# Adjacency times signs, with residual and layer norm: quadrants' statistics combined by ScalarE copies and VectorE aggregation in place of TensorE sums

## The chip, the cores and the metric

The kernel runs on one core of one Trainium2 chip. The metric is the time of the program on the device in microseconds (us), lower is better. Runs of one kernel spread by some per cent here: the three of the kernel before go from 1036.94 to 1065.42.

## What is computed

```
x: (8192, 256)  adj: (8192, 8192), all float32, about 3 entries a row besides zeros  weight: (256, 256)
bw = sign(weight);  ba = max(sign(x), 0)
xw = ba @ bw.T                       # (8192, 256), small whole numbers
out = relu(adj @ xw)                 # the large product
y = x + out
result = (y - mean(y)) / sqrt(var(y) + 1e-5)     # over the 256 columns of each row
```

The product reads 268 MB of adj. It is made in two parts, hi and lo: hi is adj rounded to the matmul's type fp32r, lo the rest, and both are multiplied by xw and added up in the same bank.

## The kernel before, in words

The 8192 output rows are 16 blocks of 512 (`NBLK`, `b`). For each block the 8192 columns of adj are 8 chunks (`CH`), each of which is loaded by 4 DMAs of 512 KB, one to each quadrant of 32 partitions; a chunk is 4 units (`UPC`), so a block has 32 units (`UB`). Within a block `u` is the unit's number, `n` is counted over all blocks. Four chunk buffers (`SLOTS`) stand in `raw`.

One unit goes through this chain: VectorE transposes it in 32x32 squares (`turn`, L478), into `turned` (four buffers) or, for the ten "V" units of a block, into two PSUM banks; ScalarE converts it to hi (`make_hi`, L359); lo = turned - hi is made by GpSimd for the 22 "P" units (L339) and by VectorE for the V units (`make_lo`, L482); TensorE multiplies (`use_unit`, L685), 8 matmuls of 512 columns. hi and lo are rings of 6 (`RING`): `make_hi(n)` waits until TensorE has used unit n - 6. The V units are u = 0, 4, 7, 10, 13, 16, 20, 23, 26, 29 (in the first block 1 and 12 differ). Block b's sums stand transposed in two of four banks, which of the two pairs alternates with b.

The end of a block runs under the next block's units (`ending(b, u)`, b the finished block, u the unit of the one that runs). Each engine's order is the order of the code: unit's work first, then what `ending` has for that u. On VectorE: u = 7 transposes the two banks into `relu` (L511), u = 8 takes relu and adds the rows of x (L515), u = 9 to 12 make 16 `bn_stats`, four in each (L520). The rows are spread in quadrants: a partition holds 64 of a row's 256 columns (`rows_q`), so each row's statistics stand in four quadrants and have to be combined. TensorE does that after its unit 8 (`add_means`, L753: four matmuls with the matrix `quads`, which adds up over quadrants) and after its unit 16 (`add_vars`, L761), with small VectorE steps between (L524, L528, L532). ScalarE takes the root at u = 23 (L375), VectorE makes the scale and shift at 25 and 26 (L536, L539), and ScalarE normalises 16 groups of 64 columns, four in each of u = 27 to 30 (L380). `add_means` waits for all 16 `bn_stats`, on an engine whose order is fixed, so the products of unit 9 stand behind that wait.

DMAs are issued by SyncE (SP, the lower two quadrants of everything) and ScalarE (ACT, the upper two). Adjacency: `start_chunk`, L207; ScalarE issues one quadrant after unit n = 4(ch - 3) and the other one unit later. Rows of x are loaded by `load_quads` (L265, at u = 20 on ScalarE, behind a block's chunk 0 on SyncE) and the result stored by `store_quads` (L270, at u = 31 on ScalarE, behind chunk 3 on SyncE), 128 KB a quadrant, in packets of 256 bytes; the adjacency goes in packets of 1 KB. The last block is normalised in another way (`PIECES`), which the change leaves as it is.

## Time and profile before

| | us |
|---|---|
| median of 3 runs | 1051.39 |
| lowest, highest | 1036.94, 1065.42 |
| profiled execution | 1054.38 |
| its span, first to last instruction | 1052.6 |

| engine | busy us | share of the span |
|---|---|---|
| TensorE (PE) | 998.0 | 95% |
| its weight loads (PEld) | 819.0 | 78% |
| VectorE (DVE) | 898.8 | 85% |
| GpSimd (POOL) | 855.0 | 81% |
| ScalarE (ACT) | 638.7 | 61% |

The profile is that of one execution. Busy time is what an engine spends in instructions; two matmuls overlap in it, so TensorE's share is not a share of its peak, and the start of one matmul to the start of the next is the better measure. An instruction of TensorE, VectorE, ScalarE or GpSimd is named by engine, line and operation, output <- inputs. ACTq and SPq are the engines' own queues, in which a DMA's issue has a duration too. "Granted clock" is the share of TensorE's full clock of 2.4 GHz; 0.50 is its other level, 1.2 GHz. The rows of the sections below are printed as the profile has them.

### The profile page before, as it was taken

How to read it: one execution, taken by the hardware profiler on the slowest of the kernel's cores; microseconds unless marked ns; L12 is line 12 of the kernel's file. 1: busy time of each engine (PE TensorE's matmuls, PEld its weight loads, DVE VectorE, ACT ScalarE, POOL GpSimd, SP SyncE). 2: the span in 40 equal slices, each digit the busy share in tenths (PEclk: the TensorE clock that was granted, in tenths of full speed). 3: DMA queues.
4: the chain of work that ended last, by engine and by line, in shares of the span. 5: the costliest groups of instructions: out<-in, count | busy, mean ns of one | idle time of the engine just before them, and what ended most of it. 6: DMA issues, size and time to landing. Idle time of an engine off the chain costs nothing.

```text
span 1052.6 us, 12987 instructions
## 1 busy us (share of the span) xinstructions
PE 998.0 (95%) x4612; PEld 819.0 (78%) x4612; DVE 898.8 (85%) x1080; ACT 638.7 (61%) x807; POOL 855.0 (81%) x362
## 2 busy tenths in 40 slices
PE   6989999999999999999999999899998999999997
PEld 5978787887878787787877878688786887778776
DVE  6768979889898988979898897978979888798895
ACT  4777575565857457475665756547475664746565
POOL 3658978898898888879888897878879887888894
PEclk9999999999999999999999999999999999989999
DMA  9999999999999999999999999999999999999991
GB/s 303 349 331 324 272 298 291 267 308 277 301 284 299 294 258 282 274 293 292 289 316 258 292 282 288 280 244 289 277 292 290 281 295 274 274 269 263 304 205 40
DMA packets 344225, 294.74 MB, mean 280 GB/s; under 512 B 72544, under 2 KB 344160, under 8 KB 344160
## 3 DMA queue, kind: packets, MB, share of 16 engines
q1 hardware_dynamic: 172480, 147.35, 55.0%
q10 hardware_dynamic: 171680, 146.56, 53.9%
q8 instruction: 36, 0.59, 0.3%
q14 instruction: 29, 0.24, 0.1%
HBM read 285.47 MB, written 8.39 MB: 279 GB/s over the span
## 4 chain that ended last, share of the span: by engine, by line
DVE 34%; PE 34%; ACTq 11%; ACT 11%; issue 9%; POOL 0%; DVEq 0%; POOLq 0%
PE ps L685 29%; DVE turned L478 10%; DVE lo L482 9%; ACTq L207 8%; ACT hi L359 7%; DVE ps L478 7%; DVE stats_q L520 3%; ACTq L265 2%; ACT rows_e L380 2%; PE ps L679 2%; DVE relu L511 2%; DVE rows_e L515 1%; DVE rows L515 1%; ACT rows L380 1%; DVE dev_q L532 1%
## 5 line engine op out<-in xcount | busy, mean ns | idle before, releaser
L339 POOL TENSOR_TENSOR lo<-turned,hi 128x1024 fp32r<-128x1024 f32 x351 | 851.8, 2449 | 170.3 <-ACT hi L359 168.8
L685 PE MATMUL ps<-hi,xw 128*128 128x512 f32 x1984 | 786.5, 396 | 9.4 <-POOL lo L339 6.3
L685 PE MATMUL ps<-lo,xw 128*128 128x512 f32 x1984 | 780.3, 393 | 0.0
L359 ACT ACTIVATE hi<-turned 128x1024 fp32r<-128x1024 f32 x351 | 370.3, 1059 | 344.6 <-DVE turned L478 231.2
L685 PEld LDWEIGHTS ps<-hi,xw 128*128 128x128 f32 x1984 | 377.5, 190 | 96.7 <-POOL lo L339 15.0
L685 PEld LDWEIGHTS ps<-lo,xw 128*128 128x128 f32 x1984 | 377.3, 190 | 77.7
L478 DVE STREAM_TRANSPOSE turned<-raw 128x1024 f32<-128x1024 f32 x351 | 427.0, 1220 | 1.1 <-DMA raw<-in_adj_dram 1.1
L482 DVE TENSOR_TENSOR lo<-ps,hi 128x1024 fp32r<-128x1024 f32 x161 | 195.4, 1214 | 126.2 <-ACT hi L359 125.6
L478 DVE STREAM_TRANSPOSE ps<-raw 128x1024 f32<-128x1024 f32 x161 | 196.8, 1223 | 3.3 <-DMA raw<-in_adj_dram 3.0
L359 ACT ACTIVATE hi<-ps 128x1024 fp32r<-128x1024 f32 x161 | 164.5, 1022 | 42.2 <-DVE ps L478 30.8
L380 ACT ACTIVATE rows_e<-rows_e,shift_q,rstd_q 128x64 f32<-128x64 f32 x128 | 45.5, 428 | 0.0
L380 ACT ACTIVATE rows<-rows,shift_q,rstd_q 128x64 f32<-128x64 f32 x112 | 39.8, 428 | 0.0
L753 PE MATMUL ps<-stats_q,quads 128*128 128x16 f32 x60 | 10.4, 288 | 29.7 <-DVE stats_q L520 29.7
L753 PEld LDWEIGHTS ps<-stats_q,quads 128*128 128x128 f32 x60 | 8.9, 214 | 36.0 <-DVE stats_q L520 33.4
L679 PE MATMUL ps<-hi,xw 128*128 128x256 f32 x96 | 25.2, 300 | 0.1
L679 PE MATMUL ps<-lo,xw 128*128 128x256 f32 x96 | 24.6, 293 | 0.0
L532 DVE SCALAR_TENSOR_TENSOR dev_q<-sq_q,stats_q 128x32 f32<-128x32 f32 x15 | 24.5, 1631 | 0.0
L352 ACT ACTIVATE xw<-ps 128x1024 fp32r<-128x1024 f32 x16 | 16.4, 1025 | 9.8 <-PE ps L661 8.3
L679 PEld LDWEIGHTS ps<-hi,xw 128*128 128x128 f32 x96 | 19.4, 202 | 0.3 <-issue 0.3
L679 PEld LDWEIGHTS ps<-lo,xw 128*128 128x128 f32 x96 | 19.5, 203 | 0.0
L661 PE MATMUL ps<-sign_wT,rows 128*128 128x256 bf16 x128 | 17.9, 286 | 0.9 <-DVE rows L451 0.9
L511 DVE STREAM_TRANSPOSE relu<-ps 128x1024 f32<-128x1024 f32 x15 | 18.1, 1207 | 0.0
(54 smaller groups left out, 202.0 us busy)
## 6 DMA issues: line engine op xcount, KB each, us to landing
raw<-in_adj_dram SPq DMA_DIRECT2D x250, 512.0 KB, 10.8
raw<-in_adj_dram ACTq DMA_DIRECT2D x250, 512.0 KB, 12.6
raw<-in_adj_dram SPq DMA_DIRECT2D x12, 256.0 KB, 9.0
raw<-in_adj_dram ACTq DMA_DIRECT2D x12, 256.0 KB, 9.4
x_sb<-in_x_dram SPq DMA_DIRECT2D x10, 256.0 KB, 11.2
x_sb<-in_x_dram ACTq DMA_DIRECT2D x10, 256.0 KB, 11.6
rows_e<-in_x_dram ACTq DMA_DIRECT2D x16, 128.0 KB, 12.8
rows_e<-in_x_dram SPq DMA_DIRECT2D x16, 128.0 KB, 11.2
```

The lines of the kernel that those rows point to most:

```text
L207: eng.dma_start(raw_view(ch)[g * Q:(g + 1) * Q], adj_v[ch // CH, ch % CH, g]).then_inc(adj_loaded[ch % SLOTS], 16)
L265: eng.dma_start(rows_q[b % 2][q * Q:(q + 1) * Q], x_quads[b, q]).then_inc(quads_loaded[b % 2], 16)
L339: pool.tensor_tensor(lo[:, n % RING], turned[:, ordinal(n) % TP], hi[:, n % RING].bitcast(f32), ALU.subtract).then_inc(p_los_made, 1)
L359: act.activation(hi[:, n % RING], src, ACT.Copy).then_inc(his_made, 1)
L380: done = act.activation(row, row, ACT.Identity, bias=shift_q[:, t:t + 1], scale=rstd_q[:, t:t + 1])
L478: dve.transpose(dst.rearrange("p (k t j) -> p k t j", k=uk, j=Q), src).then_inc(units_turned, 1)
L482: dve.tensor_tensor(lo[:, n % RING], turned_v[:, :], hi[:, n % RING].bitcast(f32), ALU.subtract).then_inc(v_los_made, 1)
L511: dve.transpose(flat[0].rearrange("p (t a j) -> p a t j", t=NT, a=DH), pair[b % 2]).then_inc(sums_turned, 1)
L520: dve.bn_stats(stats_q[:, t], rows_q[b % 2][:, t]).then_inc(stats_made, 1)
L532: dve.scalar_tensor_tensor(out=dev_q[:], in0=sq_q[:], scalar=float(Q), in1=parts, op0=ALU.mult, op1=ALU.add).then_inc(parts_made, 1)
L679: return pe.matmul(acc[b % 2][a][:, n0:n0 + MB // 2], xw[:, step, a * P:(a + 1) * P], part[:, n % RING, k * MB // 2:(k + 1) * MB // 2], st ...
L685: return pe.matmul(acc[b % 2][a], xw[:, step, a * P:(a + 1) * P], part[:, n % RING, k * MB:(k + 1) * MB], start=(step == 0 and part is hi) ...
```

## The change

The line numbers of the changed kernel are some 15 lower on TensorE and some 8 higher on VectorE.

- TensorE's `add_means` and `add_vars`, the matrix `quads` and the small steps L524, L528 and L532 are gone.
- relu is taken by ScalarE in the banks themselves, after its hi of unit 5, two activations of 512 columns. VectorE transposes the banks at u = 6 (L518), not 7, and waits for that relu. At u = 7 the rows are added (L522) by a plain add.
- The 16 `bn_stats` are made two in each of u = 8 to 15 (L527).
- At u = 16 ScalarE copies the four quadrants' statistics side by side into partitions 0 to 31 (`near`, four copies of 16 x 6 numbers, L378). At u = 17 to 20 VectorE aggregates them, 16 `bn_aggr` on 24 numbers (L531). At u = 21 ScalarE takes the root and negates the mean (L381, L382), at u = 22 and 23 VectorE makes the reciprocal and the shift (L534, L538), at u = 24 ScalarE copies both back to all four quadrants (`scale_q`, four copies, L386).
- ScalarE normalises two or three groups in each of u = 25 to 31 (L391).
- SyncE alone loads and stores rows, four quadrants each time; ScalarE issues none.

```diff
+                if u == RING - 1:
+                    act.wait_ge(units_used, (b + 1) * UB)
+                    for a in range(DH):
+                        act.activation(acc[b % 2][a], acc[b % 2][a], ACT.Relu).then_inc(relus_made, 1)
+                if u == 16:
+                    act.wait_ge(stats_made, (b + 1) * NT)
+                    for q in range(G):
+                        act.activation(near[:, :, q], stats_q[q * Q:(q + 1) * Q], ACT.Copy).then_inc(stats_near, 1)
+                if u == 21:
+                    act.wait_ge(mvs_near, (b + 1) * NT)
+                    act.activation(std_q, mv_q[:, :, 1], ACT.Sqrt, bias=eps[0:Q]).then_inc(stds_made, 1)
+                    act.activation(neg_q, mv_q[:, :, 0], ACT.Copy, scale=-1.0).then_inc(negs_made, 1)
+                if u == 24:
+                    act.wait_ge(fins_made, b + 1)
+                    for q in range(G):
+                        act.activation(scale_q[q * Q:(q + 1) * Q], fin_q, ACT.Copy).then_inc(fins_spread, 1)
+                if u >= 25:
+                    act.wait_ge(fins_spread, (b + 1) * G)
+                    for t in range(NT * (u - 25) // 7, NT * (u - 24) // 7):
-                if u == 31:
-                    store_quads(act, b, UPPER)
-                if n % UB == 20 and n // UB < NBLK - 1:
-                    load_quads(act, n // UB, UPPER)
...
-                    dve.scalar_tensor_tensor(out=rows_q[b % 2], in0=back_q, scalar=0.0, in1=rows_q[b % 2],
-                                             op0=ALU.max, op1=ALU.add).then_inc(sums_made, 1)
-                if 9 <= u < 13:
+                    dve.tensor_tensor(rows_q[b % 2], flat[0].rearrange("p (t c) -> p t c", t=NT), rows_q[b % 2],
+                                      ALU.add).then_inc(sums_made, 1)
+                if 8 <= u < 16:
...
+                if 17 <= u < 21:
+                    dve.wait_ge(stats_near, (b + 1) * G)
+                    for t in range((u - 17) * G, (u - 16) * G):
+                        dve.bn_aggr(mv_q[:, t], near[:, t].rearrange("p q s -> p (q s)")).then_inc(mvs_near, 1)
...
-                if n >= UB and n % UB == MEANS_AT:
-                    add_means(n // UB - 1)
-                if n >= UB and n % UB == VARS_AT:
-                    add_vars(n // UB - 1)
```

TensorE's order at the end of unit 8 of the second block, before: the last products of unit 8, the matmuls of `add_means`, the first product of unit 9.

```order
L685 MATMUL ps<-hi,xw 128x512
L685 MATMUL ps<-lo,xw 128x512
L753 MATMUL ps<-stats_q,quads 128x16 x2
L685 MATMUL ps<-hi,xw 128x512
L685 MATMUL ps<-lo,xw 128x512
```

The L753 row, and after unit 16 an L761 row like it, stand nowhere in the changed order: unit 9 follows unit 8 directly.

VectorE's order from the transposition of the banks on (L511; `turned` and `ps` are the two places that L478 writes), before:

```order
L511 STREAM_TRANSPOSE relu<-ps 128x2x16x32 [waits sums_made,units_used]
L478 STREAM_TRANSPOSE turned<-raw 128x1024 [waits p_los_made,adj_loaded2]
L482 TENSOR_TENSOR lo<-ps,hi 128x1024 [waits his_made]
L515 SCALAR_TENSOR_TENSOR rows_e<-relu,rows_e 128x1024 [waits quads_loaded0,sums_turned]
L478 STREAM_TRANSPOSE turned<-raw 128x1024 [waits p_los_made]
L520 BN_STATS stats_q<-rows_e 128x6 [waits sums_made]
L520 BN_STATS stats_q<-rows_e 128x6 x3
L478 STREAM_TRANSPOSE ps<-raw 128x1024 [waits v_los_made]
```

And the same place now:

```order
L518 STREAM_TRANSPOSE relu<-ps 128x2x16x32 [waits fins_spread,relus_made]
L486 STREAM_TRANSPOSE ps<-raw 128x1024 [waits v_los_made]
L522 TENSOR_TENSOR rows_e<-relu,rows_e 128x1024 [waits quads_loaded0,sums_turned]
L486 STREAM_TRANSPOSE turned<-raw 128x1024 [waits p_los_made,adj_loaded2]
L490 TENSOR_TENSOR lo<-ps,hi 128x1024 [waits his_made]
L527 BN_STATS stats_q<-rows_e 128x6 [waits sums_made]
L527 BN_STATS stats_q<-rows_e 128x6
L486 STREAM_TRANSPOSE turned<-raw 128x1024 [waits p_los_made]
```

The transposition stands one unit earlier and waits for relus_made, and two statistics stand behind a unit where four stood.

ScalarE's order at the end of a block and the start of the next (units 30, 31, 0, 1; rows at the top and the stores L270 of two quadrants), before:

```order
L380 ACTIVATE rows_e<-rows_e,shift_q,rstd_q 128x64 [waits shifts_made]
L380 ACTIVATE rows_e<-rows_e,shift_q,rstd_q 128x64 x3
L359 ACTIVATE hi<-turned 128x1024 [waits units_used,units_turned]
L270 DMA out_0_dram<-rows_e 32x16x64 [waits blocks_done]
L270 DMA out_0_dram<-rows_e 32x16x64
L359 ACTIVATE hi<-ps 128x1024 [waits units_used,units_turned]
L207 DMA raw<-in_adj_dram 32x16x256
L359 ACTIVATE hi<-turned 128x1024 [waits units_used,units_turned]
L207 DMA raw<-in_adj_dram 32x16x256
```

And now:

```order
L391 ACTIVATE rows_e<-rows_e,scale_q 128x64 [waits fins_spread]
L391 ACTIVATE rows_e<-rows_e,scale_q 128x64
L357 ACTIVATE hi<-turned 128x1024 [waits units_used,units_turned]
L391 ACTIVATE rows_e<-rows_e,scale_q 128x64 [waits fins_spread]
L391 ACTIVATE rows_e<-rows_e,scale_q 128x64 x2
L357 ACTIVATE hi<-ps 128x1024 [waits units_used,units_turned]
L205 DMA raw<-in_adj_dram 32x16x256
L357 ACTIVATE hi<-turned 128x1024 [waits units_used,units_turned]
L205 DMA raw<-in_adj_dram 32x16x256
```

The two stores have left ScalarE; the normalisation reaches into unit 31.

## Rows read from the trace of the kernel before

**Rows 1.** The page's busy times, and the view of cores with the mean clock.
```profile
PE 998.0 (95%) x4612; PEld 819.0 (78%) x4612; DVE 898.8 (85%) x1080; ACT 638.7 (61%) x807; POOL 855.0 (81%) x362
core 0: 1052.6 us, clock 0.984
```
**Rows 2.** Windows: length, PE, PEld, DVE, ACT, POOL busy, clock, DMA, GB/s.
```profile
200.00:240.00 40.00, 40.00 (x178) 33.13 (x177) 33.85 (x39) 26.80 (x39) 36.62 (x15) 1.00 1.13 310
118.40:1002.50 884.10, 850.09 (x3699) 693.32 (x3699) 774.27 (x925) 535.41 (x688) 748.39 (x309) 0.98 1.13 283
```
**Rows 3.** Waits of PE and PEld: us in total, times, longest.
```profile
PE ps L753 <- DVE stats_q L520: 29.7, 15, 2.3
PE ps L685 <- POOL lo L339: 6.3, 15, 0.9
...
PEld ps L685 <- POOL lo L339: 15.0, 21, 1.3
```
**Rows 4.** Timeline of PE around an L753 and an L761: start, us, instruction.
```profile
115.84 0.39 PE L685 MATMUL ps<-lo,xw 128*128 128x512 f32 x1
118.42 0.59 PE L753 MATMUL ps<-stats_q,quads 128*128 128x16 f32 x4 [2.19 <-DVE stats_q L520]
...
133.47 0.51 PE L761 MATMUL ps<-dev_q,quads 128*128 128x16 f32 x4
133.84 0.48 PE L685 MATMUL ps<-hi,xw 128*128 128x512 f32 x1
```
**Rows 5.** Windows around a fall of the clock, columns as in rows 2.
```profile
178.40:181.20 2.80, 0.51 (x4) 0.09 (x2) 2.80 (x11) 1.10 (x2) 2.17 (x1) 1.00 1.12 290
182.40:185.80 3.40, 3.40 (x9) 2.63 (x8) 3.40 (x4) 2.02 (x3) 3.02 (x2) 0.50 1.12 214
```
**Rows 6.** Timeline of ACT and its queue, end of block 5.
```profile
402.72 1.43 ACT L380 ACTIVATE rows_e<-rows_e,shift_q,rstd_q 128x64 f32<-128x64 f32 x4
...
404.17 0.93 ACTq L270 DMA_DIRECT2D out_dram<-rows_e  x2
...
405.22 3.28 ACTq L207 DMA_DIRECT2D raw<-in_adj_dram  x1
```
**Rows 7.** Lines L207 and L270: issue ns min/median/max, first and last start.
```profile
L207 ACTq DMA_DIRECT2D raw<-in_adj_dram x250: 317/318/4184, 26.6 to 1009.3; - x125
...
L270 SPq DMA_DIRECT2D out_dram<-rows_e x16: 327/1990/3446, 155.3 to 1036.7; - x16
```
**Rows 8.** Groups by line, shapes apart: busy us, mean ns, idle before.
```profile
L532 DVE SCALAR_TENSOR_TENSOR dev_q<-sq_q,stats_q 128x32 f32<-128x32 f32 x15 | 24.5, 1631 | 0.0
...
L515 DVE SCALAR_TENSOR_TENSOR rows<-relu,rows 128x1024 f32<-128x1024 f32 x7 | 13.8, 1970 | 0.0
...
L528 DVE TENSOR_TENSOR sq_q<-dev_q 128x32 f32<-128x32 f32 x15 | 2.8, 184 | 0.0
```
**Rows 9.** Timeline at the kernel's end: one row of ACT, one of DVE.
```profile
1037.99 1.09 ACT L424 ACTIVATE relu<-ps 128x512 f32<-128x512 f32 x2 [0.76 <-PE ps L685]
...
1044.67 0.25 DVE L493 BATCH_NORM_AGGREGATE mv<-stats 128x2 f32<-128x6 f32 x2
```
**Rows 10.** The page's DMA issues: KB each, median us to landing.
```profile
raw<-in_adj_dram SPq DMA_DIRECT2D x250, 512.0 KB, 10.8
raw<-in_adj_dram ACTq DMA_DIRECT2D x250, 512.0 KB, 12.6
```
**Rows 11.** DMA view of 171:177, 182:185 and 204:207; packets, MB, share.
```profile
q1 hardware_dynamic: 1052, 1.04, 55.2%
...
DMA packets 649, 0.64 MB, mean 214 GB/s; under 512 B 22, under 2 KB 649, under 8 KB 649
...
q1 hardware_dynamic: 537, 0.53, 94.1%
...
q1 hardware_dynamic: 973, 0.36, 61.0%
```
**Rows 12.** Timeline of POOL: the subtraction for unit 12 of that block.
```profile
118.95 2.41 POOL L339 TENSOR_TENSOR lo<-turned,hi 128x1024 fp32r<-128x1024 f32 x1 [0.41 <-ACT hi L359]
```

More of the change, by code:

```diff
@@ L43, in build @@
     C4 = D // G
-    MEANS_AT, VARS_AT = 8, 16
     TAIL = 4
@@ L111, in build @@
         shift = sb("shift", [P, MT], f32)
-        quad = sb("quad", [P, Q], f32)
-        quads = sb("quads", [P, P], f32)
         stats_q = sb("stats_q", [P, NT, 6], f32)
-        dev_q = sb("dev_q", [P, NT, 2], f32)
-        sq_q = sb("sq_q", [P, NT, 2], f32)
-        std_q = sb("std_q", [P, NT], f32)
-        rstd_q = sb("rstd_q", [P, NT], f32)
-        shift_q = sb("shift_q", [P, NT], f32)
+        scale_q = sb("scale_q", [P, 2, NT], f32)
         eps = sb("eps", [P, 1], f32)
         warm = sb("warm", [P, 1], f32)
+        in0 = relu.rearrange("p a b -> p (a b)")[0:Q]
+        near = in0[:, 0:NT * G * 6].rearrange("p (t q s) -> p t q s", t=NT, q=G)
+        mv_q = in0[:, 384:384 + NT * 2].rearrange("p (t e) -> p t e", t=NT)
+        std_q, neg_q = in0[:, 416:416 + NT], in0[:, 432:432 + NT]
+        fin_q = in0[:, 448:448 + NT * 2].rearrange("p (e t) -> p e t", e=2)
         rows_q = [rows_e[:], rows[:].rearrange("p m d -> p (m d)").rearrange("p (t c) -> p t c", t=NT)]
@@ L135, in build @@
         pair = [ps[:, 2 * h * BANK:(2 * h + 2) * BANK].rearrange("p (a t r) -> p a t r", a=DH, t=NT) for h in range(2)]
-        sum_means, sum_vars = (ps[:, b * BANK:b * BANK + NT] for b in (6, 7))
         back = ps[:, 6 * BANK:8 * BANK].rearrange("p (m d) -> p m d", m=MT)
@@ L177, in build @@
         sums_turned = sem("sums_turned")
[L178 to L184 removed]
+        relus_made = sem("relus_made")
+        stats_near = sem("stats_near")
+        mvs_near = sem("mvs_near")
+        negs_made = sem("negs_made")
+        fins_made = sem("fins_made")
+        fins_spread = sem("fins_spread")
         relus_turned = sem("relus_turned")
@@ L254, in start_rest_of_halved, with load_quads @@
                 start_half(eng, 5, side[1:2])
-        def load_quads(eng, b, side):
+        def load_quads(eng, b):
             if b >= 2:
@@ L263, in load_quads, with store_quads @@
                 eng.wait_ge(xw_made, GROUPS)
-            for q in side:
+            for q in range(G):
                 eng.dma_start(rows_q[b % 2][q * Q:(q + 1) * Q], x_quads[b, q]).then_inc(quads_loaded[b % 2], 16)
-        def store_quads(eng, b, side):
+        def store_quads(eng, b):
             eng.wait_ge(blocks_done, b + 1)
-            for q in side:
+            for q in range(G):
                 eng.dma_start(out_quads[b, q], rows_q[b % 2][q * Q:(q + 1) * Q]).then_inc(quads_stored[b % 2], 16)
@@ L518, in ending @@
+                if 8 <= u < 16:
                     dve.wait_ge(sums_made, b + 1)
-                    for t in range((u - 9) * G, (u - 8) * G):
+                    for t in range((u - 8) * 2, (u - 7) * 2):
                         dve.bn_stats(stats_q[:, t], rows_q[b % 2][:, t]).then_inc(stats_made, 1)
-                if u == 16:
-                    dve.wait_ge(means_summed, b + 1)
-                    for e in range(2):
-                        last = dve.tensor_tensor(dev_q[:, :, e], stats_q[:, :, 1 + 3 * e], sum_means, ALU.subtract)
-                    last.then_inc(devs_made, 1)
@@ L542, in make_quads @@
-            def make_quads():
-                dve.wait_ge(idents_made, 2)
-                dve.tensor_reduce(quad[:], ident[:].rearrange("p (q r) -> p r q", q=G), mybir.AxisListType.X,
-                                  ALU.add).then_inc(quad_made, 1)
-                dve.wait_ge(quad_made, 1)
-                for q in range(G):
-                    last = dve.tensor_scalar(quads[:, q * Q:(q + 1) * Q], quad[:], 1.0 / (G * 2), None, ALU.mult)
-                last.then_inc(quads_made, 1)
+                    dve.wait_ge(negs_made, b + 1)
@@ L743, in turn_piece @@
                             last.then_inc(relus_turned, 1)
-            def add_means(b):
-                if b == 0:
-                    pe.wait_ge(quads_made, 1)
-                pe.wait_ge(stats_made, (b + 1) * NT)
-                if b:
-                    pe.wait_ge(shifts_made, b)
-                for e in range(2):
-                    last = pe.matmul(sum_means, quads[:], stats_q[:, :, 1 + 3 * e], start=(e == 0), stop=(e == 1))
-                last.then_inc(means_summed, 1)
-            def add_vars(b):
-                pe.wait_ge(parts_made, b + 1)
-                if b:
-                    pe.wait_ge(stds_made, b)
-                for e in range(2):
-                    last = pe.matmul(sum_vars, quads[:], dev_q[:, :, e], start=(e == 0), stop=(e == 1))
-                last.then_inc(vars_summed, 1)
             turn_step(0)
```

60 lines of the change are left out of this document (19 added, 41 removed).

## The prediction

> **What bounds the kernel now.** I read the busy table first: TensorE is busy 95% of the span, its mean clock 0.984 of full [rows 1]. Then one stretch with nothing but products, 200 to 240 us: 178 matmuls touch it, two of them begun before it, so one starts every 40.00 / 176.4 = 0.227 us [rows 2]. A block is 32 units of 8, so 256 x 0.227 = 58.1 us. It really takes 63.15: fourteen blocks lie between the first and the last L753, 884.1 / 14 [rows 2]. TensorE bounds the kernel, and 5.0 us a block, 75 us over the 15 blocks that carry an ending, are no products. Where they are:
>
> 1. The waits: TensorE waits 29.7 us, in 15 times, for the last of L520's statistics before L753 [rows 3]. The timeline shows one: a product starts at 115.84, the next thing at 118.42 [rows 4].
> 2. The small matmuls themselves: 0.59 for the four of L753, and 0.37 from the first of L761 to the next product [rows 4], 0.96 x 15 = 14.4 us.
> 3. The clock. 0.016 of 1052.6 us is 16.8 us lost; about 1.5 of it is the idle end, so 15.3. From 182.4 to 185.8 the granted clock is 0.50, the 1.2 GHz level, and 9 matmuls fit where 3.4 / 0.227 would give 15 at 2.4 GHz [rows 5]. Just before, from 178.4 to 181.2, TensorE stood still but for 0.51 us: an L753 wait. I take these stalls as the cause of the falls.
> 4. Waits of L685 for GpSimd's lo: 6.3 us by TensorE's count, 15.0 by that of its weight loads [rows 3]. I take 10. An example of what is behind them is on ScalarE: after its two row stores at 404.17 the next adjacency issue takes 3.28 us [rows 6], where the median one takes 0.318 [rows 7], and the next hi conversion stands behind it.
>
> 29.7 + 14.4 + 15.3 + 10 = 69 us, near the 75 from the pace.
>
> **The change, part by part.**
>
> *TensorE* loses both groups of small matmuls and the waits in front of them; it waits for no statistic any more: items 1 and 2, -44.1. With no standstill of over 2 us left in the steady part the clock has no cause to fall: item 3, -15.3.
>
> *VectorE* is busy 774.27 / 14 = 55.3 us a block [rows 2]. Removed: L532 (1.63 in the mean), L528 (0.18) [rows 8] and three no larger than it, L524 twice and L539 (0.1 each of engine time): -2.1. Added: 16 aggregations of 24 numbers; the nearest row is L493 with 6 numbers, 0.25 for two, so 0.12 to 0.2 each, 2 to 3.2 [rows 9]; I take 2.0. The product L538 has two small SBUF inputs, as L528 (0.18) and L532 (1.63) have; I take 1.6, since like L532 it stands between transpositions. L515 (1.97 [rows 8]) becomes a plain add of the same 1024 numbers; at best it loses as much as L532 is longer than L528, 1.4 us, at worst nothing; I take no gain. The transposition of the banks waits for ScalarE's relu, which follows hi of unit 5: hi and relu are 2.1 us, a transposition 1.15, so VectorE may stand up to 1 us; +0.6. Sum 55.3 - 2.1 + 2.0 + 1.6 + 0.6 = 57.4 (55.5 to 59.3) of 58.1 us. It fits, with little to spare.
>
> L532 takes 1.63 us for 32 numbers a partition, L528 0.18 [rows 8]. The Trainium skill ("SBUF — State Buffer", the practical consequences of its ports) says that a VectorE instruction with two SBUF inputs contends with a GpSimd instruction that reads SBUF, and that the second to issue blocks until the first is done. By it L538 could wait for a whole GpSimd subtraction, 2.4 us here, and the 57.4 become 58.2. L532 agrees with the rule, L528 does not.
>
> *ScalarE* is busy 535.41 / 14 = 38.2 us a block [rows 2]. Relu of two banks adds 1.1 [rows 9], and nine small copies at most 0.33 each (four rows of L380 take 1.43 [rows 6]) 3.0: 42 of 58.1, cost nothing. Each stands behind a hi conversion and is shorter than the pause until the ring frees the next place. The normalisation goes from four rows behind each of four units, 0.95 + 1.43 = 2.4 us and so over TensorE's 1.81, to two or three rows behind seven units, 0.95 + 2.3 x 0.33 = 1.7. And ScalarE issues no rows: what made its adjacency issues long is gone. For both -10 us (item 4).
>
> *SyncE* issues eight row transfers a block in place of four, at some 2.0 us each [rows 7], and adjacency issues stand behind them. Chunks are issued 12 units, 21.8 us, before use and land after 10.8 us from SyncE and 12.6 from ScalarE [rows 10], so SyncE's side can be 8 us late. But its queue now carries 16 x 512 KB and 8 x 128 KB a block. With both queues full each moves 1.04 MB in 6 us, 174 GB/s; SyncE's nearly alone moves 0.53 MB in 3 us, 177, with 214 in sum [rows 11]. So a queue gives 175 GB/s whoever else works. 8192 packets of 1 KB at 175 a us are 46.8 us. In a window of mostly short packets 973 pass in 3 us [rows 11], 324 a us; at that rate the 4096 short ones are 12.6 us, and somewhat less without the long ones among them: 10.5 to 12.6. Together 57.3 to 59.4 of 58.1 us: full, where it was 52 of 63.15. That is a limit, not hidden work; I price it in the sum.
>
> The Trainium skill ("DMA: Bandwidth & Descriptors", Issuing engines are not separate DMA queues) says that issuing from several engines saves only issue time, since all run on the same 16 engines. By that rule the move to SyncE costs no bandwidth and the term would be zero, 10 us less than I say. The windows with 349 (both queues) and 214 GB/s speak against it.
>
> **Sum.** 69 off would leave a block of 58.5. VectorE's work and SyncE's queue are both within a microsecond of that, so they will not always be on time: 0.7 us a block, 10 us back. The profiled execution took 1054.4 us, 1052.6 of it span; 1054.4 - 69 + 10 = 995. The median of the runs, 1051.4, is 3 below it in a spread of 28 us. I say 994.
>
> **The rivals.**
>
> *A, the forecast (0.58):* a block of 58.4 to 59.7, 983 to 1003.
>
> *B, VectorE or SyncE's queue becomes the bound (0.22).* With L538 at 2.4, aggregations at 0.2 and chunks landing late, a block takes 60 to 61.5: 25 to 47 saved, 1007 to 1030. For it: both sums are over 57. Against: the dear ends must fall together. It decides where either's work passes 59.5.
>
> *C, the stall only moves (0.12).* VectorE's burst in units 7 to 12 is what TensorE waited for, and its lo may be late instead. GpSimd ends lo of unit 12 at 118.95 + 2.41 = 121.36 [rows 12]; unstalled, TensorE would want it three units after 116.07, at 121.5. That is a margin of 0.1 us. If lo is late by 2 us a block, only item 2 and half of item 3 are gained, 22 us: 1032. Against: eight of the sixteen statistics move behind unit 12, 1 us, and ScalarE loses no lead at the block's end.
>
> *D, slower (0.06): rows on one queue hold up the adjacency.* Were a short packet as dear as a long one, SyncE's 12288 packets at 175 a us took 70 us a block: 15 x 7 = +105, 1158. It decides from 64.5 us of queue time. Against: the 324 packets a us.
>
> *E, no change (0.02):* stalls and clock come back for another cause.
>
> **Numbers.** Over 2% (21 us, about what a measurement of this kernel can tell) faster is under 1030: A, B and a third of C, 0.84. Within 2%: the rest of C, E: 0.10. Slower: D, 0.06. The range ends above where C does and below at the floor: 15 x 5.0 off is 979, and 3 less for the median.
>
> **What would show it.** Right: no wait of TensorE for statistics; a mean clock over 0.99; ScalarE's adjacency issues all near 0.32; L685 waiting for lo under 1 us a block; VectorE busy 95% of a block. B: VectorE hardly waits for hi any more, or waits for raw by over 1 us a block. C: L685 waits for lo by 1 to 2 us in units 10 to 15. D, and I am wrong altogether: SyncE's issues pile up and raw lands after its turn in every block. If the clock still falls without a stall before it, item 3 was misread.

## The result and the profile after

The changed kernel took 1086.62 us (median of 4 runs, 1084.72 to 1098.44), the kernel before 1056.68 beside it (4 runs): ratio 1.043, 95% interval 1.0254 to 1.0607. It is slower, and the prediction, 994 in 976 to 1033, was wrong. A ratio compares the faster executions of the two kernels (those within 1.5% of each one's fastest; of the kernel before 1036.94 and 1051.39), so it isn't the quotient of the medians. The profiled execution took 1085.55.

The page's busy times, the view of cores, and the window of [rows 2] (us, then PE, PEld, DVE, ACT, POOL busy, clock, DMA, GB/s):

```profile
PE 998.8 (92%) x4492; PEld 788.4 (73%) x4492; DVE 914.9 (84%) x1255; ACT 686.3 (63%) x972; POOL 841.8 (78%) x362
core 0: 1083.8 us, clock 0.999
118.40:1002.50 884.10, 825.79 (x3493) 646.60 (x3492) 769.76 (x1071) 567.93 (x829) 718.49 (x302) 1.00 1.13 274
```

The clock is whole, as forecast, and the same 884.1 us hold fewer products. Measured from a block's first product to the next one's, blocks 2 to 14 take 64.98 us in the mean (63.18 before, 58.1 without any stall). The waits (us in all, times, longest) say what for:

```profile
DVE ps L486 <- DMA raw<-in_adj_dram: 103.0, 29, 6.9
...
PE ps L671 <- POOL lo L337: 37.4, 95, 1.3
PE ps L671 <- DVE lo L490: 30.7, 27, 2.2
```

No wait for a statistic is left, where [rows 3] had 29.7 us. Instead VectorE waits for the adjacency 103.0 us, 6.9 a block, where the same instructions waited 3.0 in all before, and 58.1 + 6.9 is the block's 65.0. The waits of TensorE are what comes through of it. The timeline of SyncE's queue and of VectorE shows one place, with chunk 1 of a block:

```profile
416.42 7.43 SPq L205 DMA_DIRECT2D raw<-in_adj_dram  x2
423.89 9.76 SPq L268 DMA_DIRECT2D out_dram<-rows_e  x4
433.70 28.39 SPq L205 DMA_DIRECT2D raw<-in_adj_dram  x10
...
425.14 1.26 DVE L486 STREAM_TRANSPOSE ps<-raw 128x1024 f32<-128x1024 f32 x1 [5.49 <-DMA raw<-in_adj_dram]
```

SyncE is not free in this stretch: one issue follows the other, and four stores of rows stand 9.76 us in front of the next chunk. The lines of the issues (ns min/median/max), the first that of the kernel before, and the page's landing times after:

```profile
L207 SPq DMA_DIRECT2D raw<-in_adj_dram x250: 311/489/3862, 26.6 to 1007.2; - x125
...
L205 SPq DMA_DIRECT2D raw<-in_adj_dram x250: 311/2136/5267, 26.8 to 1040.8; - x125
L205 ACTq DMA_DIRECT2D raw<-in_adj_dram x250: 317/318/919, 26.8 to 1042.0; - x125
...
raw<-in_adj_dram SPq DMA_DIRECT2D x250, 512.0 KB, 13.4
raw<-in_adj_dram ACTq DMA_DIRECT2D x250, 512.0 KB, 11.6
```

ScalarE's long issues are gone (4184 at most in [rows 7]). SyncE's median went from 0.49 to 2.14 us and its landings from 10.8 to 13.4 [rows 10]. From 200 to 900 us SyncE spends 92% of the time in issues, 37% before.

### The profile page after: what moved, and what is told of

Its sections match the earlier page's. It is cut to its first block, busy times and chain, and to the rows that moved or that the text cites. A ratio compares the mean times of both kernels' runs of the same rounds, so it can differ in the third digit from the quotient of the medians.

```text
span 1083.8 us, 13072 instructions
## 1 busy us (share of the span) xinstructions
PE 998.8 (92%) x4492; PEld 788.4 (73%) x4492; DVE 914.9 (84%) x1255; ACT 686.3 (63%) x972; POOL 841.8 (78%) x362
## 3 DMA queue, kind: packets, MB, share of 16 engines
q1 hardware_dynamic: 204160, 155.22, 60.7%
## 4 chain that ended last, share of the span: by engine, by line
DVE 42%; DMA 34%; issue 10%; PE 5%; ACT 4%; SPq 2%; POOL 1%; ACTq 0%; POOLq 0%; DVEq 0%
DMA raw<-in_adj_dram 34%; DVE turned L486 19%; DVE ps L486 7%; DVE lo L490 7%; DVE relu L531 3%; ACT hi L357 2%; SPq L205 2%; PE ps L671 2%; DVE rows_e L522 2%; DVE relu L518 2%; PE ps L665 2%; DVE rows L522 2%; POOL lo L337 1%; DVE relu L538 1%; PE ps L647 1%
## 5 line engine op out<-in xcount | busy, mean ns | idle before, releaser
L337 POOL TENSOR_TENSOR lo<-turned,hi 128x1024 fp32r<-128x1024 f32 x351 | 838.6, 2410 | 215.3 <-ACT hi L357 208.5
L671 PEld LDWEIGHTS ps<-hi,xw 128*128 128x128 f32 x1984 | 372.4, 188 | 198.4 <-POOL lo L337 80.0
L671 PEld LDWEIGHTS ps<-lo,xw 128*128 128x128 f32 x1984 | 373.1, 188 | 73.7
L486 DVE STREAM_TRANSPOSE ps<-raw 128x1024 f32<-128x1024 f32 x161 | 197.7, 1228 | 103.2 <-DMA raw<-in_adj_dram 103.0
L391 ACT ACTIVATE rows_e<-rows_e,scale_q 128x64 f32<-128x64 f32 x128 | 47.9, 428 | 0.0
L391 ACT ACTIVATE rows<-rows,scale_q 128x64 f32<-128x64 f32 x112 | 41.9, 428 | 0.0
L531 DVE BATCH_NORM_AGGREGATE relu<-relu 32x2 f32<-32x24 f32 x240 | 35.1, 198 | 0.0
L350 ACT ACTIVATE xw<-ps 128x1024 fp32r<-128x1024 f32 x16 | 16.4, 1026 | 12.7 <-PE ps L647 11.2
L527 DVE BATCH_NORM_STATS2 stats_q<-rows_e 128x6 f32<-128x64 f32 x128 | 20.0, 194 | 0.0
L522 DVE TENSOR_TENSOR rows_e<-relu,rows_e 128x1024 f32<-128x1024 f32 x8 | 19.8, 2469 | 0.0
L665 PEld LDWEIGHTS ps<-hi,xw 128*128 128x128 f32 x96 | 19.4, 202 | 0.3 <-issue 0.3
L665 PEld LDWEIGHTS ps<-lo,xw 128*128 128x128 f32 x96 | 19.5, 203 | 0.0
L518 DVE STREAM_TRANSPOSE relu<-ps 128x1024 f32<-128x1024 f32 x15 | 18.1, 1207 | 0.0
## 6 DMA issues: line engine op xcount, KB each, us to landing
raw<-in_adj_dram SPq DMA_DIRECT2D x250, 512.0 KB, 13.4
```

Of the source, the lines that this page charges most:

```text
L337: pool.tensor_tensor(lo[:, n % RING], turned[:, ordinal(n) % TP], hi[:, n % RING].bitcast(f32), ALU.subtract).then_inc(p_los_made, 1)
L391: done = act.activation(row, row, ACT.Identity, bias=scale_q[:, 1, t:t + 1], scale=scale_q[:, 0, t:t + 1])
L486: dve.transpose(dst.rearrange("p (k t j) -> p k t j", k=uk, j=Q), src).then_inc(units_turned, 1)
L518: dve.transpose(flat[0].rearrange("p (t a j) -> p a t j", t=NT, a=DH), pair[b % 2]).then_inc(sums_turned, 1)
L522: dve.tensor_tensor(rows_q[b % 2], flat[0].rearrange("p (t c) -> p t c", t=NT), rows_q[b % 2], ALU.add).then_inc(sums_made, 1)
L531: dve.bn_aggr(mv_q[:, t], near[:, t].rearrange("p q s -> p (q s)")).then_inc(mvs_near, 1)
```

## The experiments

Two theories stood at first. **Q**: all rows on SyncE's queue make raw late. **C**: the new chain of small steps costs as much as the old. "Block" is measured as above, the clock is that of the profiled execution; a dash stands where the comparison gave no interval.

| run | us (lowest, highest) | ratio [95%] | clock | block |
|---|---|---|---|---|
| e1 after, rows on both | 1088.2 (1076.7, 1092.3) | 1.0523 [1.0378, 1.0668] | 0.992 | 65.7 |
| e2 before, rows on SyncE | 1103.5 (1096.7, 1110.9) | 1.0701 [1.0523, 1.0879] | 0.965 | 66.2 |
| e3 before, sums 2 units later | 1033.7 (1026.1, 1046.3) | 0.9928 [0.9871, 0.9985] | 0.997 | 62.3 |
| e4 after, rows in smaller groups | 1137.5 (1117.7, 1146.1) | 1.0892 [1.0592, 1.1192] | 0.952 | 68.2 |
| e5 after, bytes balanced | 1084.7 (1073.3, 1105.8) | 1.0461 [1.031, 1.0612] | 0.987 | 65.2 |
| e6 after, half of the rows | 1022.5 (1006.8, 1042.6) | – | 0.999 | 60.4 |
| e7 before, half of the rows | 1005.3 (997.6, 1052.5) | 0.9704 [0.9549, 0.9859] | 0.995 | 59.0 |
| e8 e1, load at unit 26 | 1049.0 (1044.8, 1057.7) | 1.0164 [1.0054, 1.0273] | 0.989 | 62.7 |
| e9 before, single row issues | 1008.0 (996.1, 1019.0) | 0.9716 [0.9538, 0.9893] | 0.992 | 60.0 |
| e9 again | 1023.9 (1010.4, 1031.1) | 0.9839 [0.9712, 0.9966] | 0.986 | 61.5 |
| e12 before, upper rows on GpSimd | 1078.5 (1074.4, 1083.5) | 1.0483 [1.0342, 1.0625] | 0.976 | 65.0 |
| e13 after with e9's issues | 1053.2 (1010.5, 1061.4) | – | 0.999 | 63.4 |
| e14 after, one row issue a chunk | 1140.2 (1114.3, 1166.8) | – | 0.990 | 67.3 |
| e16 e13, other units | 1012.0 (1004.2, 1021.8) | 0.9787 [0.9632, 0.9943] | 0.999 | 59.9 |
| e16 again | 1008.9 (992.8, 1020.2) | 0.9617 [0.9532, 0.9702] | 0.999 | 59.0 |
| e17 after, rows' bytes halved | 1095.3 (1088.0, 1099.9) | 1.056 [1.0487, 1.0632] | 0.990 | 66.1 |
| e18 after, rows' packets halved | 1032.1 (1017.5, 1038.8) | – | 0.997 | 60.7 |
| e19 e9 and e3 together | 999.7 (996.2, 1023.6) | 0.9628 [0.9575, 0.968] | 0.992 | 61.1 |

### Is it the rows on SyncE?

e2 makes that part of the change alone, in the kernel before:

```diff
-                        load_quads(sp, b - 1, LOWER)
+                        load_quads(sp, b - 1, range(G))
...
-                        store_quads(sp, b - 2, LOWER)
+                        store_quads(sp, b - 2, range(G))
...
-                    store_quads(act, b, UPPER)
...
-                    load_quads(act, n // UB, UPPER)
```

> The kernel before with only the row transfers moved to SyncE. Theory Q: the two late chunks a block come with it, VectorE waits 80 us or more for raw, 1085 to 1140 us. Theory C: nothing but ScalarE's relief, 1035 to 1055 us.

It took 1103, +7%. Its waits:

```profile
DVE ps L474 <- DMA raw<-in_adj_dram: 138.4, 32, 10.6
...
PE ps L749 <- DVE stats_q L516: 41.8, 14, 3.4
```

The same waits for raw appear without anything else of the change. Q holds. The stall at the statistics' sum is there too, larger than before (41.8 us), although ScalarE issues no rows; VectorE's lead is lost there too, I take it by the late raw. e1 undoes that part in the changed kernel:

```diff
-                        load_quads(sp, b - 1)
+                        load_quads(sp, b - 1, LOWER)
...
+                        store_quads(act, b, UPPER)
...
+                if n % UB == 20 and n // UB < NBLK - 1:
+                    load_quads(act, n // UB, UPPER)
```

> The changed kernel with its rows issued by SyncE and ScalarE again, two quadrants each, as before the change. Theory Q (rows on SyncE's queue are the whole loss): raw no longer lands late, VectorE's waits for raw fall from 103 us to under 10, and the statistics part keeps its gain: 990 to 1015 us, 0.94 to 0.965 of the kernel before, clock over 0.99. Theory C (the new chain on VectorE and ScalarE costs what the stall had cost): 1040 to 1090 us, with L671's waits for lo still at 70 us or more.

Under Q this had to be fast, and it was a miss: 1088, the number of C. Raw is on time, but the timeline of ScalarE and its queue shows a new wait:

```profile
403.53 4.25 ACTq L263 DMA_DIRECT2D rows<-in_x_dram  x2
...
407.90 3.03 ACTq L205 DMA_DIRECT2D raw<-in_adj_dram  x1
410.98 0.31 ACT L381 ACTIVATE relu<-relu,eps 32x16 f32<-32x16 f32 x1 [2.03 <-issue]
```

The root of unit 21 stands behind the issues of units 20 and 21, and VectorE, which wants it at unit 22, stands too (51.0 us, 14 times, longest 4.3). So both are true of the two placements: on SyncE the rows make raw late, on ScalarE at unit 20 they hold a step of the new chain. e8 moves the load away from it (`n % UB == 20` becomes `26`).

> Run e1 (changed statistics, rows on both engines) with ScalarE's row loads at unit 26 in place of 20. In e1 VectorE waited 51 us for ScalarE's root, which stood behind those loads and the long issue after them. If that was e1's loss, these waits go and the time falls by 30 to 50 us to 1035 to 1055. If ScalarE's blocked time counts wherever it stands, other waits take their place and the time stays over 1070.

As expected (1035 to 1055): the wait for the root is gone and the time is 1049. What is left are TensorE's waits for GpSimd's lo, 38.3 us.

### Order or capacity, packets or bytes?

e4 and e5 were the first attempts to relieve SyncE. e4 issues rows behind chunks 0 to 5 in groups of one, one and two; e5 hands one SyncE quadrant of chunks 1 and 4 to ScalarE:

```diff
-                start_chunk(sp, ch, LOWER)
+                start_chunk(sp, ch, LOWER[0:1] if ch % CH in (1, 4) else LOWER)
...
+                    if ch >= CH and ch % CH in (1, 4) and n == issue_at(ch, 1) + 1:
+                        start_chunk(act, ch, LOWER[1:2])
```

> The changed kernel with rows on SyncE alone, but spread: one or two quadrants behind each of chunks 0 to 5 in place of four behind chunk 0 and four behind chunk 3. If the burst is what makes chunks 1 and 4 late, VectorE's waits for raw fall below 30 us and the time to 1000 to 1035. If the queue as a whole cannot carry 24 issues a block (my sum: 57 to 59 us), other chunks come late in their place and the time stays at 1060 to 1090.

> The changed kernel (rows on SyncE alone), with one of SyncE's two adjacency quadrants of chunks 1 and 4 issued by ScalarE instead, one unit after its own second. Each queue then has the bytes of before. Theory of the late queue: VectorE's waits for raw fall from 103 to under 40 us, the time to 1010 to 1050 us. If 18 issues are too many for ScalarE, its adjacency issues grow long again (over 1 us in the mean) and the time stays over 1065.

e4 was slower, 1137, but the rows themselves now came late (VectorE's waits at L522: 66.7 and 51.6 us), so it tells nothing of the order alone. e5 changed nothing (1085, and 102.1 us of waits for raw, where under 40 were expected): two issues of 24 are gone, but those left take 2.78 us each where they took 2.48, and the remaining quadrant of chunk 1 still stands behind four row issues.

e14 removes the piece of four without making the rows late; each row issue goes behind a chunk of its own:

```diff
+                    if c < 2:
+                        load_quads(sp, b - 1, range(c + 2, c + 3))
+                    if 3 <= c < 7 and b >= 2:
+                        store_quads(sp, b - 2, range(c - 3, c - 2))
+                    if c >= 6 and b < NBLK - 1:
+                        load_quads(sp, b, range(c - 6, c - 5))
```

> The changed kernel, with SyncE alone issuing the same eight row transfers a block, but never four in a row: one behind each of the eight chunks (loads of the next block's rows behind chunks 6, 7, 0 and 1, stores behind chunks 3 to 6). Theory O (order: four row issues standing together put 9.8 us in front of the next chunk, 6.9 us of which VectorE waits for): at most 2.5 us now stand in front of any chunk, the waits for raw fall from 103 us to under 45, and the time to 1030 or less. Theory S (capacity: 24 issues a block are more than SyncE's queue can carry beside the adjacency): raw stays late by as much, only in more and shorter waits, and the time is 1045 to 1090.

It took 1140, 50 us past the range of Theory S and far from that of O: rows standing four in a row are not the cause. VectorE's waits, and a part of the timeline of SyncE:

```profile
DVE ps L493 <- DMA raw<-in_adj_dram: 98.9, 52, 4.5
DVE turned L493 <- DMA raw<-in_adj_dram: 41.8, 32, 3.1
...
516.35 2.68 SPq L264 DMA_DIRECT2D rows<-in_x_dram  x1
519.07 5.04 SPq L205 DMA_DIRECT2D raw<-in_adj_dram  x2
524.16 2.34 SPq L264 DMA_DIRECT2D rows<-in_x_dram  x1
526.54 4.54 SPq L205 DMA_DIRECT2D raw<-in_adj_dram  x2
```

The waits are shorter, more frequent and 140.7 us in all. SyncE is in issues 99% of 200 to 900 us, 24 x 2.78 = 66.7 of a block's 67.3 us. Its queue carries 12288 packets of data a block: 183 a us here, 189 in the changed kernel, 186 in e2 (in issues 92 and 93% of the time). I take that for what the queue can carry of this mix.

It is no constant of the queue. With 11264 packets a block (e5) SyncE is in issues 93% of the time at 173 a us, and with 10240, as many as before the change, 94% in e12 (158 a us), 85% in e6 and 82% in e7 (all three below), against 37% in the kernel before. In each of these, as in the changed kernel, ScalarE's queue carries fewer packets than in the kernel before. So the length of SyncE's issues depends on more than its own packets; on what else, no run here takes apart.

The Trainium skill ("Perfetto Trace Analysis", What "DMA-bound" means) lists this picture, an issuing engine's track that is solid with DMAs, as a bound of its own, and says that large descriptors are what matters then. The next two runs agree as far as they go: fewer packets help and shorter ones don't. No run has larger packets.

e17 and e18 ask what the capacity is of. Both halve the rows' bytes from the third block on, e17 by shorter packets, e18 by fewer. The loads' edit, of e17 and of e18 (the stores' is like it):

```diff
+                if b >= 2:
+                    into, frm = into[:, :, 0:32], frm[:, :, 0:32]
```

```diff
+                if b >= 2:
+                    into, frm = into[:, 0:8], frm[:, 0:8]
```

> The changed kernel, but from the third block on each row transfer carries only the first 32 of the 64 columns (the other half of the result is not stored): as many packets as before the edit, each of 128 bytes, so half of the rows' bytes. Theory P (SyncE's queue is bounded by packets, about 185 a us, whatever their size from 128 to 1024 bytes: 12288 packets took 64.98 us in the changed kernel and 67.3 with single issues): no better, 1070 to 1095, waits for raw 80 us or more. Theory B (bytes decide): 8.4 MB less on a queue of 155 MB is 5%, so 1030 to 1055.

> The changed kernel, but from the third block on each row transfer carries only eight of its sixteen groups of rows (the others are not stored): the same bytes as in the run with 128-byte packets, but half the packets, of 256 bytes; still eight issues a block on SyncE. Theory P (packets): 10240 a block at 185 a us are 55.4 us, no longer the bound; 1005 to 1040 and waits for raw under 45 us. Theory B (bytes): the same time as with 128-byte packets, within 1%. Theory I (the number of issues counts, each costing SyncE its two us or more): both near 1087.

SyncE's queue on the page (packets, MB) and VectorE's wait, first of e17, then of e18:

```profile
q1 hardware_dynamic: 204160, 147.88, 58.2%
DVE ps L489 <- DMA raw<-in_adj_dram: 118.0, 32, 8.9
```

```profile
q1 hardware_dynamic: 175488, 147.88, 57.2%
DVE ps L489 <- DMA raw<-in_adj_dram: 49.7, 24, 6.1
```

The same bytes, the same number of issues, and 1095 against 1032: the difference is that of the packets. (e18's waits for raw, 49.7 us, are a little over the 45 of Theory P.) Halving the bytes gave nothing, so 128 or 256 bytes make no difference; taking 2048 short packets of 12288 off a block took 5.4 us off it. At 186 a us they would be 11 us. Part of the difference may be that at 10240 packets the queue no longer decides alone, since TensorE needs 58.1; that isn't shown. How dear a short packet is beside one of 1 KB is therefore only estimated: 5.4 / 2048 = 2.6 ns or more by these two runs, (65.0 - 46.8) / 4096 = 4.4 ns by what long ones at 175 a us leave of the changed kernel's block; a long one at that rate takes 5.7.

e6 and e7 leave the upper quadrants' rows out (loaded for the first two blocks, never stored), for the chain of after and of before. The loads' edit of e6 (e7 does the same where SyncE loads, and drops ScalarE's loads and stores):

```diff
-            for q in range(G):
+            for q in (range(G) if b < 2 else LOWER):
```

> The changed kernel with only the lower two quadrants of the rows loaded and stored (the upper two are loaded for the first two blocks and never stored, so half of the result is missing). SyncE then issues as many rows as before the change and ScalarE none. Theory L (the new statistics chain is fine; the loss is only in who issues rows): raw in time as before the change, L671 waits for lo under 15 us, 985 to 1008 us. Theory C (the new chain costs by itself): over 1025 us with L671 waiting for lo by 40 us or more.

> The kernel before with the same: rows of the upper two quadrants neither loaded (but for the first blocks) nor stored, so ScalarE issues no rows and SyncE as many as before. Theory L: ScalarE's long issues after rows were what took VectorE's and GpSimd's lead, and the stall at L753 only showed it; L753's waits fall from 30 to under 12 us and the time to 1000 to 1022 us. Rival: the stall is VectorE's burst of statistics, waits stay at 25 to 30 us and the time at 1035 or more.

e6, again 10240 packets, takes the block of e18: 60.4. It missed both of its ranges: 1022 us, 24 us of TensorE's waits for lo, and raw not in time as before the change: VectorE waits 41.8 us for it, with no more packets on SyncE than the kernel before has. That is the open point above.

e7 answers another question: what TensorE's waits before came from. All of its waits at the statistics' sum:

```profile
PE ps L749 <- DVE stats_q L516: 3.4, 1, 3.4
```

29.7 us in 15 waits [rows 3] have become one in the first block, and later blocks take 59.0 us, the 58.1 of products and the 0.9 of small matmuls. The chain and TensorE's place in it are untouched: the stall of the kernel before came with ScalarE's rows, not from the chain alone. The run takes off those rows' traffic with their issues; e9 below keeps the traffic and moves the issues.

### Where can the rows go?

e3 treats only the symptom: `MEANS_AT, VARS_AT = 8, 16` becomes `10, 18`.

> The kernel before with TensorE's two groups of small matmuls two units later (after units 10 and 18). TensorE then reaches them 3.6 us later than VectorE's last statistics are due, so L753's 30 us of waits go. If the stalls are what lets the clock fall, the clock is over 0.99 too and the time 1005 to 1022 us. If the clock falls by itself, it stays at 0.98 and the time is 1022 to 1035. If VectorE's burst makes lo late instead (rival C of the prediction), L685 waits for lo by 25 us or more and the time stays over 1035.

The wait for statistics is gone and the clock rises to 0.997, as the first theory says, but the time, 1034, is in the second one's range: the gain is small, since the stall turns up as a wait for lo (`PE ps L685 <- POOL lo`: 30.2 us; 6.3 before).

e9 treats the cause: each engine issues its own rows, never two in one place; ScalarE loads after units 18 and 22 and stores after units 2 and 6 of the next block.

```diff
-                if n % UB == 20 and n // UB < NBLK - 1:
-                    load_quads(act, n // UB, UPPER)
+                if n % UB in (18, 22) and n // UB < NBLK - 1:
+                    i = (n % UB - 18) // 4
+                    load_quads(act, n // UB, UPPER[i:i + 1])
+                if n >= 2 * UB and n % UB in (2, 6):
+                    i = (n % UB - 2) // 4
+                    store_quads(act, n // UB - 2, UPPER[i:i + 1])
```

> The kernel before with its row transfers taken apart: never two row issues in a row. ScalarE loads one quadrant at unit 18 and one at 22, stores one at unit 2 and one at 6; SyncE one behind each of chunks 0 and 1 (loads) and 3 and 4 (stores). If ScalarE's long issues come from bursts (rows and adjacency in flight together), its adjacency issues fall from 15 us a block to under 8, L753's waits under 20 us, and the time to 1005 to 1035 us. If only the number of issues counts, nothing changes: 1035 to 1055.

> The kernel before with its row transfers issued one at a time, ScalarE's at units 18, 22, 2 and 6. The earlier reading was 1008.0, 0.9716 of before [0.9538, 0.9893]. If the single issues and not the chip of that call made the gain, this comes out at 0.96 to 0.98 again, 1005 to 1025, with under 12 us of TensorE's waits for statistics; if it was chance, within 2% of before with waits over 20 us.

0.9716, then 0.9839: faster by 1.6 to 2.8%, with 9.1 and 22.7 us of waits for statistics left (under 12 were expected the second time). So where the issues stand is part of the stall. ScalarE's adjacency issues still take 12.2 and 14.4 us a block (17.0 in the kernel before), where under 8 were expected. e12 gives the upper rows to GpSimd instead.

> The kernel before with the upper two quadrants' rows loaded and stored by GpSimd (loads at unit 20, stores at unit 3 of the next block) instead of ScalarE. ScalarE's adjacency issues are then all near 0.32 us, as in e7. If GpSimd's issues cost it little, the stall at L753 goes and the time is 1000 to 1025 us. If an issue costs GpSimd a microsecond or more, its 22 subtractions of 2.4 us leave 5 us a block for it and L685 waits for lo by 30 us or more: 1040 to 1090.

```profile
DVE ps L484 <- DMA raw<-in_adj_dram: 110.2, 42, 8.6
...
q0 software_dynamic: 2880, 7.87, 2.7%
```

Raw is late again, though SyncE's queue carries no more than before. The time, 1078, is in the second range, but not for its reason: L692 waits 12 us for lo in all. e7, in which nobody transfers those rows, has 9.0 us of this wait, so it comes with GpSimd's 2880 packets; how stays open.

e13 puts e9's row issues under the changed chain.

> The changed statistics with the rows issued as in e9. Against e9 it tells what the new chain of ScalarE and VectorE is worth once nobody's queue blocks. If the chain is as good as TensorE's sums, the two are within 1%; by my own sum of VectorE's work (57.4 of 58.1 us a block against 55.3) it is up to 2% slower than e9: 1010 to 1050 us.

1053 in the median, a little over the range, with VectorE's wait at the banks' relu 32.0 us, 14 times, and its wait for the root 16.4 in the profiled execution (1057): the stores after units 2 and 6 stand around the relu after unit 5, the loads after 18 and 22 around the root. e16 moves ScalarE's loads to units 26 and 30 and its stores to 7 and 11, behind every step for which VectorE waits.

> The changed kernel with ScalarE issuing the upper quadrants' rows one at a time, loads behind units 26 and 30, stores behind units 7 and 11 of the next block: away from the units 5, 16, 21 and 24 at which VectorE waits for a step of ScalarE's. The same chain with single issues at 18, 22, 2 and 6 took 1053, with 32 us of VectorE's waits for relu. If those waits, ScalarE's long issues standing in front of a step that VectorE is waiting for, are all that is wrong with the changed chain: 1005 to 1025 and the waits for relu under 8 us. If the chain itself costs more than TensorE's sums did: 1040 to 1060, with the waits for lo as before.

> The changed chain with ScalarE's single row issues at units 26, 30, 7 and 11, again: 1012.0 and 0.9787 [0.9632, 0.9943] the first time. If the chain itself costs nothing: 1005 to 1020, and within 1% of the kernel before with its rows placed likewise.

1012 and 1009, 0.9787 and 0.9617, with 13.3 and 7.3 us of waits for relu (under 8 expected). One of e13's four executions took 1010 as well, the others 1050 to 1061, so how much of the time the new places save is not certain; the waits are what shows it. Cores and VectorE's and TensorE's waits of the second:

```profile
core 0: 991.0 us, clock 0.999
DVE relu L525 <- ACT ps L374: 7.3, 9, 1.3
DVE ps L493 <- DMA raw<-in_adj_dram: 3.4, 3, 1.8
PE ps L678 <- POOL lo L337: 6.1, 19, 0.4
```

Six blocks of it take 58.0 us: products and nothing else (the mean is 59.0). The new chain costs nothing there once ScalarE's issues stand clear of it, and C falls.

e19 joins e9 and e3 for the kernel before.

> The kernel before with single row issues (ScalarE's at units 18, 22, 2 and 6) and its sums over quadrants made two units later, after units 10 and 18. The single issues alone left 9 to 23 us of waits for statistics and a clock of 0.986 to 0.992. If the two edits answer different things: no wait for statistics, clock 0.998, and 990 to 1010. If the stall only moves to lo, as it did when the sums alone were moved: 1010 to 1030, with waits for GpSimd's lo over 15 us.

999.7, 0.9628 [0.9575, 0.968], beside e16's 0.9617 [0.9532, 0.9702]: the two edits add up, and the two chains, each with its rows placed for it, can't be told apart. Both beat both kernels. e19's profiled execution took 1023.6, so its rows say only that no wait for statistics is left and that in such an execution TensorE waits 16.4 us for GpSimd's lo.

## Why the prediction was wrong, by its own steps

**TensorE, items 1 and 2: right.** No small matmul, no wait for statistics. That most of the gain is there to be had is shown by e16, the changed chain with the upper rows back on ScalarE: medians of 1012 and 1009, and blocks of 59.9 and 59.0 where the kernel before takes 63.18. Its fastest execution, 992.8, is below the forecast's 994, which was meant for the median.

**The clock, item 3: right.** 0.999 after; 0.997 in e3, whose only edit is the place of the sums, so the falls went with the stall in front of them.

**VectorE: right in the sum, wrong in its parts.** 769.76 of 884.1 us at 64.98 a block is 56.6, where 57.4 less 0.6 of waiting was said. The groups by line:

```profile
L531 DVE BATCH_NORM_AGGREGATE relu<-relu 32x2 f32<-32x24 f32 x240 | 35.1, 198 | 0.0
...
L522 DVE TENSOR_TENSOR rows_e<-relu,rows_e 128x1024 f32<-128x1024 f32 x8 | 19.8, 2469 | 0.0
...
L538 DVE TENSOR_TENSOR relu<-relu 32x16 f32<-32x16 f32 x15 | 10.1, 674 | 0.0
```

The aggregations are 2.3 us a block (2.0 said); the product 0.67 in the mean (1.6 said; one reached 2.34); the plain add takes 2.47 where the scalar_tensor_tensor took 1.97 [rows 8], so the lower bound, that it might be cheaper, was on the wrong side. The sum came out because these misses cancel.

The add and the product share a cause that the prediction half saw. It took L532 for a case of an operation that stands behind a GpSimd subtraction and L528 for a counterexample. The traces show the ends of the two engines' instructions tied together. The quick L522 and a slow one, each with the subtraction that ran when it started, then the longest L538 with its own:

```profile
167.81 2.41 POOL L337 TENSOR_TENSOR lo<-turned,hi 128x1024 fp32r<-128x1024 f32 x1
169.82 1.48 DVE L522 TENSOR_TENSOR rows<-relu,rows 128x1024 f32<-128x1024 f32 x1
...
235.78 2.40 POOL L337 TENSOR_TENSOR lo<-turned,hi 128x1024 fp32r<-128x1024 f32 x1
236.78 2.47 DVE L522 TENSOR_TENSOR rows_e<-relu,rows_e 128x1024 f32<-128x1024 f32 x1
...
140.16 2.41 POOL L337 TENSOR_TENSOR lo<-turned,hi 128x1024 fp32r<-128x1024 f32 x1
140.25 2.34 DVE L538 TENSOR_TENSOR relu<-relu 32x16 f32<-32x16 f32 x1
```

All 15 of L522, and all 15 of L515 before, end 1.08 to 1.09 us after the subtraction's end; L538 ends 0.02 to 0.03 us after it, L532 0.06. So the plain add is not dearer than the scalar_tensor_tensor: it starts earlier in a subtraction and waits longer. L528 is no counterexample: in 8 of 15 cases it meets only the last 0.13 to 0.14 us of a subtraction, and in the others none was running.

**ScalarE: right.** 567.93 us give 41.7 a block (42 said), and no adjacency issue over 0.92 us. But the item's -10 was drawn from waits that in the kernel before are only part of what the row issues cost. The prediction took VectorE's burst of statistics for the cause of the L753 stall (rival C) and ScalarE's issues for item 4 alone; e7 shows the issues behind both. The sum was not hurt, since the change removes them too.

**SyncE's queue: the step that failed.** "at that rate the 4096 short ones are 12.6 us". The 324 packets a us came from one 3 us window. Such windows exist after, too, and the DMA view shows what surrounds them: 436 to 440, 440 to 444, and a whole block, 424 to 489.

```profile
q1 hardware_dynamic: 1272, 0.33, 41.0%
...
q1 hardware_dynamic: 446, 0.29, 36.9%
...
q1 hardware_dynamic: 12280, 9.05, 62.6%
```

318 packets a us, then 112; over the block 189. The burst is followed by a gap. The mean over a block is what the queue carried, and 12288 packets took 65 to 67 us and not 57.3 to 59.4. The two parts behind it went with it: "SyncE's side can be 8 us late" counted the landing but not the queue of issues in front (9.76 us in one piece), and +10 us for the term should have been +103, by the waits for raw. This term alone, a tenth of its size, turned the sign.

That is rival D, given 0.06. Its price of 70 us a block took short packets as dear as long ones at 175 a us. The block's 65 to 67 lie between this and the forecast's 57.3 to 59.4, and 64.98 is just past the 64.5 from which it said the queue decides. Which of the forecast's two prices was too low, that of the long packets or of the short, is not settled: its 3.1 ns for a short one (1 / 324 us) lies between the two estimates behind e18. A rate that holds for 3 us was taken for one of 65. Its sign came too: raw lands after its turn in every block, with chunks 1 and 4. What spoke against it was the 3 us window alone. The sum: 69 off, as said, and 103 back in place of 10 give 1054 - 69 + 103 = 1088; 1086 was measured. That it meets so closely is partly luck: where raw is in time, in e16's two profiled executions, 48 and 62 us came off and not 69.

**The rule.** The Trainium skill ("DMA: Bandwidth & Descriptors", Issuing engines are not separate DMA queues) says that several issuing engines save only issue time, usually small. e14 and e16 again move the same bytes in the same packets, 1140 against 1009. SyncE is in issues 99% of the time in the one and 50% in the other, so the saving shows as issue time, and here it is anything but small. But the two queues together also carry more, 347 packets a us against 304. The runs don't tell which comes first, so they don't decide whether issue time is all that a second engine saves.

**Still open.** What makes an issue take 2.1 to 2.8 us, why fewer packets (e5) made the rest dearer, and why SyncE's issues are long in e6 and e7 with the packets of the kernel before, no view shows. The order may have a part in e5, where 11264 packets went at 173 a us; it wasn't measured apart. One rival for the limit is untested: but for e5, SyncE's queue carries all of the adjacency's lower two quadrants and ScalarE's all of the upper two, so a limit of a queue and one of the partitions it fills look alike. For the step from before to after it isn't needed, since each quadrant receives the same in both.

## What to carry to other kernels

Before rows, masks or other small transfers are moved to one issuing engine, count packets a period for each queue as well as bytes, and divide by the rate over a whole period, never by a burst's; then look whether that engine's issues still leave it idle time. Where an engine both computes and issues, put single issues behind steps that nobody waits for: issues in pairs at the wrong units cost the kernel before part of its stall and some 2 to 3% of its time (e9). And a wait names the last link only: take out the suspected cause (e7) before the chain is rebuilt.

## What the runs showed of the hardware

- An adjacency issue takes 0.31 us at its shortest and up to 5.27 us (SyncE, after) or 4.18 us (ScalarE, before). The engine starts nothing meanwhile: in e1 ScalarE's row issues end at 407.78 and its next conversion starts at 407.88.
- SyncE's queue, in the mean of blocks 2 to 14, carried at most 189 packets of data a us in these runs. In 4 us it carried 318 a us, in the next 4 us 112. Halving short packets from 256 to 128 bytes gained nothing; halving their number took 5.4 us off a block.
- SyncE can be in issues 82 to 94% of the time at packets a block at which, with ScalarE's queue fuller, it is at 37% (e7, e6 and e12 against the kernel before).
- Rows issued by GpSimd (2880 packets, 7.87 MB) came with 125 us of VectorE's waits for the adjacency (9.7 in e7, without those rows), and SyncE's issues rose to 3.1 us in the mean (2.4 in e7).
- A plain add of 128x1024 took 2.47 us in the changed kernel, a scalar_tensor_tensor on the same tiles 1.95 to 1.97 before; the quickest single add was 1.48. All 30 end 1.08 to 1.09 us after the end of the GpSimd subtraction that was running when they started: the place sets the time, not the operation.
